# Three edits to the slots of a fused 16-batch kernel: an early table load on ScalarE, roots moved ahead of a maximum on VectorE, unread products on TensorE

## The reference, cut to what matters

```python
edge = |conv(gray(x), scharr)| summed over two directions / 2       # 256 rows
h = concat([edge, (U * s @ Vt)[x_txt]])                             # + 128 rows of text
h = h + attention(layernorm(h))      # 16 heads of 16, causal, window of 128 keys
h = h + routed(layernorm(h))         # the 288 best rows: gelu(x @ w_block), the others x
h = h + state(layernorm(h))          # a linear recurrence over the rows, plus D * u
h = h + ffn(layernorm(h))            # shared network + 2 of 8 experts of 1024

def _ffn(x, w1, b1, w2, b2):
    h = jax.nn.gelu(x @ w1.T + b1)
    return h @ w2.T + b2
```

## Time and profile before

| | us |
|---|---|
| median of 3 runs (2033.91 to 2036.55) | 2034.94 |
| profiled execution, its own time | 2021.73 |
| profiled execution, its span | 2020.0 |
| PE busy | 1887.5 (93%) |
| DVE busy | 1395.3 (69%) |
| ACT busy | 1068.6 (53%) |
| POOL busy | 741.4 (37%) |

### The profile page before, as it was taken

One profiled execution on the slowest core, in us unless ns is written; L12 is line 12 of the kernel. 1 busy time (PEld: TensorE's weight loads), 2 busy tenths in 40 slices (PEclk: granted clock), 3 DMA queues, 4 the chain that ended last, 5 costly groups with the idle time before them and its releaser, 6 DMA issues.

```text
span 2020.0 us, 46113 instructions
## 1 busy us (share of the span) xinstructions
PE 1887.5 (93%) x14343; PEld 1639.6 (81%) x14344; DVE 1395.3 (69%) x3963; ACT 1068.6 (53%) x2511; POOL 741.4 (37%) x1074
## 2 busy tenths in 40 slices
PE   5769999999999999999999999888999999999997
PEld 5557787777777877777778777677999999999997
DVE  6768778777787787787877876764765565655653
ACT  1545556556555565565555655622655555645643
POOL 2003334233333342333333322314554454555554
PEclk9889999999999999999999999988999999999999
DMA  4321131220211312202213122012432332423322
GB/s 141 86 49 51 30 73 37 51 70 25 64 52 29 72 38 50 70 25 64 52 28 72 39 49 55 9 58 69 140 92 42 47 90 43 90 44 88 48 46 39
DMA packets 81148, 117.04 MB, mean 58 GB/s; under 512 B 20964, under 2 KB 61508, under 8 KB 78724
## 3 DMA queue, kind: packets, MB, share of 16 engines
q1 hardware_dynamic: 54372, 84.16, 15.6%
q0 software_dynamic: 23360, 27.91, 8.4%
q10 hardware_dynamic: 3312, 3.94, 0.7%
HBM read 51.58 MB, written 26.71 MB: 39 GB/s over the span
## 4 chain that ended last, share of the span: by engine, by line
PE 68%; DVE 11%; issue 10%; ACT 4%; POOL 3%; SPq 1%; ACTq 1%; DVEq 0%; POOLq 0%; DMA 0%
PE ps L1996 15%; PE ps L1800 6%; PE ps L2007 5%; PE ps L1813 5%; PE ps L2008 5%; PE ps L2009 5%; PE ps L1728 3%; PE ps L1632 3%; PE ps L1717 2%; PE ps L1718 2%; PE ps L1790 2%; PE ps L1851 2%; DVE mx L1215 2%; PE ps L1785 2%; PE ps L1666 2%
## 5 line engine op out<-in xcount | busy, mean ns | idle before, releaser
L849 ACT ACTIVATE prob<-ps,mx 128x256 f32<-128x256 f32 (+1 forms) x768 | 295.7, 445 | 125.6 <-DVE mx L1215 112.7
L969 ACT ACTIVATE hid_hi<-ps,b 128x256 fp32r<-128x256 f32 x408 | 205.8, 504 | 276.3 <-PE ps L1996 276.3
L1215 DVE TENSOR_REDUCE mx<-ps 128x2 f32<-128x512 f32 (+1 forms) x384 | 228.7, 597 | 152.2 <-PE ps L1718 124.9
L841 ACT ACTIVATE pT<-ps 128x512 f32<-128x512 f32 (+1 forms) x384 | 203.5, 535 | 191.2 <-PE ps L1728 190.3
L1562 DVE TENSOR_TENSOR hid_lo<-hid_full,hid_hi 128x256 fp32r<-128x256 f32 x408 | 171.2, 426 | 143.6 <-ACT hid_full L972 143.0
L762 POOL DMA_INDIRECT result<-yb,idx_o x102 | 179.9, 1763 | 164.0 <-DVE yb L1579 147.5
L2007 PE MATMUL ps<-w_hi,hid_hi 128*128 128x256 f32 x816 | 230.0, 282 | 0.0
L2008 PE MATMUL ps<-w_lo,hid_hi 128*128 128x256 f32 x816 | 225.5, 276 | 0.0
L2009 PE MATMUL ps<-w_hi,hid_lo 128*128 128x256 f32 x816 | 225.3, 276 | 0.0
L1728 PE MATMUL ps<-ident,prob 128*128 128x128 f32 x1280 | 208.7, 278 | 5.5 <-ACT prob L849 5.4
L972 ACT ACTIVATE hid_full<-ps,b 128x256 f32<-128x256 f32 x408 | 206.2, 505 | 0.0
(11 more groups left out here) (321 smaller groups left out, 4333.7 us busy)
## 6 DMA issues: line engine op xcount, KB each, us to landing
w_raw<-in_w SPq DMA_DIRECT2D x16, 1024.0 KB, 5.9
xin<-in_x SPq DMA_DIRECT2D x32, 384.0 KB, 3.8
ks<-k_hi SPq DMA_DIRECT2D x256, 48.0 KB, 2.1
qs<-q_hi SPq DMA_DIRECT2D x120, 96.0 KB, 2.2
ks<-k_lo SPq DMA_DIRECT2D x128, 48.0 KB, 2.1
xn_rows<-xc SPq DMA_DIRECT2D x16, 384.0 KB, 2.5
result<-h SPq DMA_DIRECT2D x16, 384.0 KB, 2.6
qs<-q_lo SPq DMA_DIRECT2D x60, 96.0 KB, 2.1
```

Source lines behind the costliest of these rows:

```text
L841: act.activation(pT[:, u % TB, :, k0:2, :], ps[:, 2 + u % 2, :].rearrange("p (h k q) -> p h k q", h=2, k=2)[:, :, k0:2, :], ACT.Copy).then ...
L849: ins = act.activation(prob[:, s % PB, hh, w], ps[:, s % 2, hh * 2 * P + w.start:(hh + 1) * 2 * P], ACT.Exp, bias=mx[:, s % 2, hh:hh + 1])
L969: act.activation(hid_hi[:, f], ps[:, f % 4, 0:CHUNK], ACT.Gelu_apprx_tanh, bias=b1[half][:, f:f + 1])
L1215: dve.tensor_reduce(mx[:, s % 2], sc, AX_X, ALU.max, negate=True).then_inc(max_done.sem, 1)
```

## The change

There are three edits.

1. On ACT, in slot 28 of each pass that has both attention and a chain (batches 1 to 15), a Gelu of one number a lane into a tile `gelu_spare` that nothing reads. It stands behind the copies of slot 27, so the load of Gelu's table is placed ahead of it, and the real Gelus find the table there.
2. On DVE, `deviations` for the chain's second norm moves from slot 8, behind the maximum, to slot 7, directly behind the statistics and ahead of the maximum.
3. On PE, in the first batch, `keep_warm` with 20 products ahead of the scores of slot 2, and with 8 behind the scores of each of the slots 3 to 14, into bank 6.

```diff
@@ scalar, sequence
                     if chain and s == TURN2:
                         turned_rows(b - 1, 2)
+                    if att and chain and s == TURN2 + 1:
+                        act.activation(gelu_spare[:], sb1[:, 0:1], ACT.Gelu_apprx_tanh)
@@ vector, chain
                 if s == RANK + NT + 3:
-                    chain_rows(b, 1)
+                    chain_rows(b, 1, True)
@@ vector, sequence
                     if att:
                         unit(b, s)
-                    if chained and s == RANK + NT + 4:
-                        dve.wait_ge(stats_ready.sem, stats_ready.at(b - 1, 2))
-                        deviations(lnc, rstd_ready, chain_step, b - 1)
@@ tensor, sequence
+                    if first and not chained and s == BLOCK:
+                        keep_warm(20, 6)
                     if att:
                         unit_scores(b, s)
+                    if first and not chained and BLOCK < s < CONV:
+                        keep_warm(8, 6)
@@ tensor, keep_warm
-            def keep_warm(count):
+            def keep_warm(count, bank=5):
                 for n in range(count):
-                    pe.matmul(ps[:, 5, 0:P], ident[:], ident[:], start=True, stop=True)
+                    pe.matmul(ps[:, bank, 0:P], ident[:], ident[:], start=True, stop=True)
```

More of the change, by code:

```diff
@@ L124, in build @@
         spare = sb("spare", [P, 1])
+        gelu_spare = sb("gelu_spare", [P, 1])
         c15 = sb("c15", [P, NT])
```

## The result

The changed kernel took 2039.41 us (median of 9 runs, 2037.29 to 2040.89), the kernel before on the same chip 2034.45 us (9 runs). The ratio is 1.0033, with a 95% interval of 1.0024 to 1.0043: 0.33% slower, about 5 to 9 us. Forecast were 2040.6 us and slower. The reader should keep an eye on that from here on.

What follows compares the result with a forecast made beforehand. PE was taken as the bound, holding 68% of the chain. The terms -6.4 + 1.8 + 1.5 + 8.8 = +5.7 us, added to the median of 2034.94 us, gave 2040.6 us, slower, with a range of 2031 to 2045.

Steps and rivals of the forecast that it cites:

- edit 1, batches 1 to 15: Early Gelu table load: removes PE's wait for the first Gelu in 14 cases, -6.4 us over the run.
- edit 2, batches 2 to 15: Early roots on DVE: `xc` and PE's transposes of it come 0.13 us later a batch, +1.8 us in 14 batches.
- edit 2, batch 1: Early roots in batch 1, without second-layer shared-network work on PE to hide behind: +1.5 us, between 0 and +2.2.
- edit 3: First batch: 116 unread products at 0.223 us each on PE's queue start slot 15 8.8 us late, all reaching batch 1.
- So PE gains its 0.46 us: Ahead of the shared network's third pair of columns: PE regains its 0.46 us idle time, not the load's 1.28 us.
- The drain of 1380 ns: At the table load: counting the skill page's drain, PE would gain 1.84 us a batch; the prediction decided against it.
- the maximum of slot 7 ends at 1034.90: DVE in the loop: with the roots ahead of it, this maximum ends then, so PE's slot 9 scores start 0.41 us late.
- The 0.79 us that DVE waited at 1033.46 is filled, but an equal wait opens ahead of slot 9: DVE in the loop: the early roots use that idle time without winning it; the net is +0.13 us a batch.
- the prediction's own sign of being wrong: Loop period falling by over 0.6 us or not at all; also slot 15 before 87, or a lower clock in before runs.
- the forecast period of 80.42 us: Loop period per batch expected after the change: 80.75 - 0.33 us, listed as a sign that the prediction was right.
- The rival in which the clock pays back: First batch: products prevent half clock on PE's stretch behind slot 15, regaining up to 11.5 us, to 2029.1 us; chance 0.22.
- The 81 ns for a matmul of 128 columns: Skill's price for the unread products: 0.16 us each, slot 15 1.7 us late, total 2033.5 us (no change); chance 0.10.

Runs made afterwards that it cites:

- e10: The kernel before, unchanged, run again on the second chip for a second profile: 2032.02 us, ratio 0.9995.
- e11: The changed kernel, unchanged, run on the second chip for a second profile, against the kernel before: 2037.68 us, ratio 1.0017.
- e12: Kernel before plus the early table load only, its unread tile at the end of the first phase's memory, moving no experts' tile: 2019.06 us, ratio 0.9938.
- e1: Kernel before plus the early table load only, its tile declared as in the change: 2021.84 us, ratio 0.9998.
- e2: Kernel before plus only the second norm's roots moved directly behind their statistics: 2027.98 us, ratio 1.0034.
- e4: Kernel before plus the early table load and the early roots, without the unread products: 2028.54 us, ratio 1.0033.
- e5: Kernel before plus only the unread products, 16 in place of 8 in each of slots 3 to 14 (212 in all): 2063.67 us, ratio 1.0156.
- e3: Kernel before plus only the 116 unread products of the first batch: 2030.09 us, ratio 1.0050.

## Why the prediction was right, and where it was not

Direction and time came out as forecast, but the sum behind them did not. The sum can be set against e10, e11 and e12, all from one chip, one profile each. Edit 1 is e12 less e10, edit 2 is e11 less e12 in the batches, the products are e11 less e10 up to `g` of batch 0.

| term | forecast | measured |
|---|---|---|
| edit 1, batches 1 to 15 | -6.4 | -0.7 - 8.9 - 1.1 = -10.7 |
| edit 2, batches 2 to 15 | +1.8 | -5.0 - 0.7 = -5.7 |
| edit 2, batch 1 | +1.5 | +2.4 |
| edit 3 | +8.8 | +10.4 |
| the experts | 0 | +9.4 |
| from the last batch to the experts | 0 | -2.0 |
| sum | +5.7 | +3.8 |

Term by term the forecast was off by -4.3, -7.5, +0.9, +1.6, +9.4 and -2.0 us, and these add up to -1.9: the total is right because they cancel, which nothing in the forecast foresaw. The timed medians of that chip differ by 3.8 us; on the chip of the prediction it was 5.0. The first agrees with the sum better than it should: the two profiled executions themselves differ by 1.2 us, since the sum leaves out the -2.6 us ahead of the ones products, and e11's lies 4.5 us below the median of its 12 runs. The stretch from the last batch to the experts has values from 71.0 to 74.8 us over all profiles, kernels of either sort among them, so its -2.0 is no effect of the change that I could show. Nor are the 2.6 us by which the stretch ahead of the ones products differs (52.1 to 55.2 us over all profiles).

**Edit 1.** The direction and the place were right. The step "So PE gains its 0.46 us" was mis-sized: it is 0.69 (e1) to 0.75 (e12 less e10). The idle figure in the earlier trace rows counts from the modelled end of the last piece of `wo`, 1004.77, but the next product doesn't wait for that end. Without the wait it starts 0.68 us behind the start of the four pieces, where 1.48 had been measured. Of these 0.80 us the pair itself takes 0.08 back (its next products start 0.54 us behind it, before 0.46). The profile of before could not have given the size: it has this pair at 1.48 us in 14 batches and at 1.01 in the last. The drain of 1380 ns, which the Trainium skill ("ScalarE: Activation LUTs", section What ACT_TABLE_LOAD costs) adds to a load, is not there in the new place either: the load starts 0.01 us after the copy ahead of it ends, and the next operation 0.02 us after the load.

**Edit 2.** The step "the maximum of slot 7 ends at 1034.90" took the eleven operations at their old lengths. One of them is 0.2 us longer in the new place, PE's scores are 0.61 us late, and +0.13 became +0.27 (e2). That is the smaller error. The larger is that the profile of before is of an execution in which DVE does not wait at slot 7, while in e10 it waits 1.56 us there, and the roots fill it. The forecast took "The 0.79 us that DVE waited at 1033.46 is filled, but an equal wait opens ahead of slot 9" from one profile alone. By this the prediction's own sign of being wrong, a period that falls by over 0.6 us, is met on the second chip (81.54 to 80.37). Where the copy is on time the forecast period of 80.42 us is near e4's 80.35; the loop of the timed executions, as far as the second chip shows it, was another one. Batch 1, with no such cover, lost 1.3 us in e2 and 2.4 here, against +1.5. The 2.4 need not be the roots' alone: the products stand ahead of them, and e5, which has products and no roots, has batch 1 1.6 us longer than e10.

**Edit 3.** Right in price and mechanism: 0.223 us read, 0.2233 measured (e5), and slot 15 39.7 us behind the ones products, where 39.5 was forecast (91.8 less 52.34). What the sum had too small is the cost against a usual execution of the kernel before: slot 15 stood 30.6 us behind them in the profile of the forecast and 29.2 to 29.9 in the eight others without the products. The rival in which the clock pays back is refuted: the clock was raised to 1.00 throughout as it says, and e3 was 8.0 us slower by its median all the same. Its condition is met nowhere: in all nine profiles without the products PE's stretch behind slot 15 has a granted clock of 1.00. By the clock page of the Trainium skill ("TensorE: Matmul & The Clock Gate", section What's actually happening) activity releases the clock, and this trace agrees (0.77 became 1.00); it was just not what PE's products waited for there. The 81 ns for a matmul of 128 columns in its section Back-to-back issue gap are not met: a piece of these fp32 products takes 112 ns, the two of a product 223 ns.

**What was missed.** The forecast gave the declaration of the new tile no term at all. It was, next to the products, the dearest part of the change, +9.4 us, and it acts in a stage that none of the three edits touches.

**The 13.2 us between the profile and the median of before.** The spans of the two profiles of the kernel before, 2020.0 and 2030.2 us (e10), differ by 10.3 us: twelve batches of 0.79 us are 9.5, the stretch ahead of the ones products adds 2.8, and batches 0, 1, 14 and 15 take 2.0 back. So some 10 of the 13.2 us are explained if the timed executions on the prediction's chip had the late copy; about 3 stay open. For it: after's profile there has it; the lowest of the nine runs of before there is 2028.90 us, far above the profiled 2021.73; and the kernel before has medians of 2032 to 2034 us on the second chip, whose profiles all have the late copy, and of 2022.12 us on the first, whose profiles all lack it. Of before's timed runs no trace exists, so this is argued and not shown.

## What to carry to other kernels

Where a profile lies 13 us below the median of the same kernel, the sum must not be built on that one execution: ask which waits it lacks. Take the idle figure ahead of a product for a lower end of what its wait costs (0.46 us here, where 0.69 to 0.75 came back), and compare distances from start to start where the trace has the same two instructions without a wait. And declare a small new tile where it moves nothing that a later, PE-bound stage reads; a tile of one column cost 9.4 us here, nearly all that the best of the three edits gained.

## What the runs showed that I had not expected

- The experts' second layer runs at 276, 279 or 281 ns a piece, 611, 616 or 620 us for the stage, according to where its tiles stand. Of the profiles, all eight without a tile ahead of them have 611; of the five with a tile of one column four have 620 and one (e1) 611, so placement sets it in most executions, not in all.
- Semaphores of PE, or what hears them, can be late by 1.0 us on ACT and 1.6 on DVE at one place of the program, in batches 2 to 13 and 15, with PE's own rows unchanged. The nine profiles that have it also record only 837 to 881 of the 1536 semaphore updates of the DMAs into `slot_rows`.
- A DVE operation on 128x3 numbers takes 0.17 us in one place and 0.32 to 0.38 in another, always the same one of eleven, in the loop (batches 2 to 13) but not in batches 1, 14 and 15, which are written out.
